# Softplus in a selective-scan kernel: a GpSimd minimum after the log for a VectorE cap before the exp, and the B and C rows copied by ScalarE

## The reference, cut to what matters

```python
def _ssm(h, in_w, xproj_w, dt_bias, A_log, Dskip, out_w):
    xz = h @ in_w
    xs, z = jnp.split(xz, 2, axis=-1)
    xs = jax.nn.silu(xs)
    proj = xs @ xproj_w
    dt = jax.nn.softplus(proj[..., :D_INNER] + dt_bias)
    Bm = proj[..., D_INNER:D_INNER + D_STATE]
    Cm = proj[..., D_INNER + D_STATE:]
    A = -jnp.exp(A_log)
    def step(hst, ins):
        dt_t, B_t, C_t, x_t = ins
        dA = jnp.exp(dt_t[:, :, None] * A)
        hst = hst * dA + (dt_t * x_t)[:, :, None] * B_t[:, None, :]
        y_t = jnp.einsum('bds,bs->bd', hst, C_t)
        return (hst, y_t)
    ...
```

## Time and profile before

| what | value |
|---|---|
| median of three runs | 3235.7 us (3233.97 to 3251.95) |
| span of the profiled execution, first to last instruction | 3238.7 us |
| time of the profiled execution beyond that span | not listed by itself |
| PE, DVE, ACT, POOL busy | 98%, 85%, 84%, 76% of the span |
| rows of the scan | 4 sequences of 128 rows |

### The profile page before, as it was taken

One profiled execution on the slowest core, in us unless ns is written; L12 is line 12 of the kernel. 1 busy time (PEld: TensorE's weight loads), 2 busy tenths in 40 slices (PEclk: granted clock), 3 DMA queues, 4 the chain that ended last, 5 costly groups with the idle time before them and its releaser, 6 DMA issues.

```text
span 3238.7 us, 59471 instructions
## 1 busy us (share of the span) xinstructions
PE 3165.7 (98%) x23272; PEld 2625.2 (81%) x23272; DVE 2754.9 (85%) x3077; ACT 2711.7 (84%) x4528; POOL 2447.2 (76%) x621
## 2 busy tenths in 40 slices
PE   7999999999999999999999999999999999999999
PEld 6998899884699889987479989998648998888844
DVE  3999999966399999996549999999656999999862
ACT  4999999955599999994569999999357999999744
POOL 2999999950199999994039999999305999999800
PEclk9999999999999999999999999999999999999999
DMA  5222322210222222220022222223002222222100
GB/s 187 72 87 68 89 68 84 87 42 1 74 66 87 79 85 74 80 88 30 9 75 72 88 83 74 86 69 92 15 14 79 84 77 84 69 74 81 48 14 7
DMA packets 194232, 222.02 MB, mean 69 GB/s; under 512 B 77336, under 2 KB 149016, under 8 KB 193056
## 3 DMA queue, kind: packets, MB, share of 16 engines
q1 hardware_dynamic: 193952, 218.22, 21.9%
HBM read 213.70 MB, written 4.48 MB: 67 GB/s over the span
## 4 chain that ended last, share of the span: by engine, by line
PE 82%; POOL 8%; issue 4%; DVE 3%; ACT 1%; DMA 1%; SPq 0%; DVEq 0%; ACTq 0%; POOLq 0%
PE bank L1053 22%; PE bank L1033 17%; PE bank L1034 10%; PE bank L933 7%; POOL states L627 5%; PE bank L1029 4%; PE bank L1252 4%; PE bank L1125 3%; POOL y_gated L627 3%; PE bank L1273 2%; PE bank L1285 2%; PE bank L1171 2%; PE bank L1352 2%; DVE states L1509 1%; PE bank L1060 1%
## 5 line engine op out<-in xcount | busy, mean ns | idle before, releaser
L627 POOL TENSOR_TENSOR states<-states,c_rows 128x2048 f32<-128x2048 f32 x336 | 1532.8, 4582 | 411.8 <-DVE states L1509 396.2
L1509 DVE TENSOR_TENSOR_SCAN states<-decay,bank 128x512 f32<-128x512 f32 x1376 | 1576.7, 1201 | 126.1 <-PE bank L1034 111.1
L780 ACT ACTIVATE decay<-dt,a_log 128x512 f32<-128x512 f32 x2048 | 1305.4, 710 | 0.0
L771 ACT ACTIVATE inflow_tok<-dtx_tok,b_tok 128x512 f32<-128x512 f32 x1536 | 995.5, 712 | 69.9 <-PE bank L1034 61.0
L1033 PE MATMUL bank<-ident,inflow_tok 128*128 128x128 f32 x5280 | 904.4, 280 | 36.6 <-DVE states L1509 18.1
L1053 PE MATMUL bank<-ident,states 128*128 128x128 f32 x5504 | 825.2, 273 | 4.4 <-DVE y_gated L1515 3.0
L1509 DVE TENSOR_TENSOR_SCAN y_gated<-decay,bank 128x512 f32<-128x512 f32 x672 | 776.3, 1201 | 12.9 <-ACT decay L780 5.5
L627 POOL TENSOR_TENSOR y_gated<-y_gated,c_rows 128x2048 f32<-128x2048 f32 x168 | 770.0, 4584 | 19.9 <-DVE y_gated L1509 18.1
L1033 PEld LDWEIGHTS bank<-ident,inflow_tok 128*128 128x128 f32 x5280 | 599.1, 141 | 207.6 <-issue 90.4
L1034 PE MATMUL bank<-b_diag,dtx_tok 128*128 128x128 f32 x3520 | 681.0, 275 | 0.0
L1053 PEld LDWEIGHTS bank<-ident,states 128*128 128x128 f32 x5504 | 645.3, 142 | 11.3 <-DVE y_gated L1515 5.3
(11 more groups left out here) (166 smaller groups left out, 2513.1 us busy)
## 6 DMA issues: line engine op xcount, KB each, us to landing
c_rows<-c_spill SPq DMA_DIRECT2D x256, 512.0 KB, 3.7
b_diag<-diag_ring SPq DMA_DIRECT2D x256, 128.0 KB, 2.2
xproj_w<-in_xproj_w SPq DMA_DIRECT2D x32, 320.0 KB, 3.9
in_w<-in_in_w SPq DMA_DIRECT2D x16, 512.0 KB, 4.6
in_w<-in_fc_w SPq DMA_DIRECT2D x8, 512.0 KB, 4.5
xproj_w<-in_w SPq DMA_DIRECT2D x8, 512.0 KB, 4.6
xproj_w<-in_fc_w SPq DMA_DIRECT2D x4, 1024.0 KB, 4.8
x_ahead<-in_x SPq DMA_DIRECT2D x4, 512.0 KB, 6.4
```

Source lines behind the costliest of these rows:

```text
L627: pool.tensor_tensor(state_row, state_row, c_row.to_broadcast([P, KI, L]), ALU.mult).then_inc(weighed, PAIRS)
L771: last_tok = act.activation(inflow_tok[:, r % SLOTS, t, :], dtx_tok[:, d, t, :], ACT.Copy, scale=b_tok[:, d, t, s:s + 1])
L780: act.activation(decay[:, r % SLOTS * KI + k, :], dt[:, d, k, :], ACT.Exp, scale=a_neg[:, d, k, s:s + 1]).then_inc(decay_ready, 1)
L1509: dve.tensor_tensor_scan(state_slots[r % STATES][:, k, time], decay[:, slot, time], banks[k % INFLOW_BANKS][:, time], 0.0, ALU.mult, ALU.a ...
```

## The change

DVE's cap in front of the exp and DVE's copy of the B and C rows are taken out. ACT copies the rows (one instruction of 512 columns behind row 26) and takes the exp straight from PSUM, with the bias as the instruction's own; the log follows in the same row. POOL then bounds the log from above with a minimum in place, one instruction of 512 columns behind rows 32, 38, 42 and 46, and the maximum on DVE, whose place in rows 33, 34, 39, 43, 47 and 48 stays, now waits for that minimum. The semaphore dt_capped is signalled by POOL in place of DVE.

```diff
-DT_CAP = 30.0
+DT_CAP = 40.0
 C_COPY_AT = 26
-C_COPY_REST_AT = 27
-DT_CAP_AT = (30, 36, 40, 44)
-DT_CAP_REST_AT = (31, 37, 41, 45)
-DT_EXP_AT = (32, 38, 42, 46)
-DT_LOG_AT = (33, 39, 43, 47)
+DT_EXP_AT = (31, 37, 41, 45)
+DT_LOG_AT = (31, 37, 41, 45)
+DT_CAP_AT = (32, 38, 42, 46)
 DT_READY_AT = (33, 39, 43, 47)
 DT_READY_REST_AT = (34, 39, 43, 48)
 DTX_AT = (34, 40, 44, 48)
...
@@ gpsimd, prepare
+                if s in DT_CAP_AT:
+                    k = DT_CAP_AT.index(s)
+                    pool.wait_ge(dt_log, n * KI + k + 1)
+                    pool.tensor_scalar(part[:, k, :], part[:, k, :], DT_CAP, None, ALU.min).then_inc(dt_capped, 1)
@@ scalar, prepare
+                if s == C_COPY_AT:
+                    act.wait_ge(c_mm, n + 1)
+                    act.activation(bc_t[:], guest[0], ACT.Copy).then_inc(c_t_ready, 1)
...
-                    act.wait_ge(dt_capped, n * KI + k + 1)
-                    act.activation(part[:, k, :], part[:, k, :], ACT.Exp).then_inc(dt_exp, 1)
+                    act.wait_ge(dt_mm, n * KI + k + 1)
+                    act.activation(part[:, k, :], guest[(k + 1) % 2], ACT.Exp, bias=dt_b[:, d, k:k + 1]).then_inc(dt_exp, 1)
@@ vector, prepare
-                    last = dve.tensor_copy(bc_t[:, c], guest[0][:, c])
...
-                            dve.wait_ge(dt_log, n * KI + k + 1)
+                            dve.wait_ge(dt_capped, n * KI + k + 1)
                         last = dve.scalar_tensor_tensor(dt[:, d, k, c], guest[(k + 1) % 2][:, c], dt_b[:, d, k:k + 1],
                                                         part[:, k, c], ALU.add, ALU.max)
...
-                            dve.wait_ge(dt_mm, n * KI + k + 1)
-                        last = dve.tensor_scalar(part[:, k, c], guest[(k + 1) % 2][:, c], dt_b[:, d, k:k + 1], DT_CAP,
-                                                 ALU.add, ALU.min)
```

More of the change, by code:

```diff
@@ L804, in batch @@
                     if d == 0 or not last:
+                        if s == C_COPY_AT:
+                            act.wait_ge(c_spilled, (b * 2 + d + 1) * 16)
                         prepare(b * 2 + d + 1, 1 - d, s)
@@ L1456, in prepare @@
                         last.then_inc(in_ready, 1)
[L1457 to L1460, removed]
-                    last = dve.tensor_copy(bc_t[:, c], guest[0][:, c])
-                    if s == C_COPY_REST_AT:
-                        last.then_inc(c_t_ready, 1)
                 for k in range(KI):
@@ L1472, in prepare @@
                             last.then_inc(dt_ready, 1)
-                    if s in (DT_CAP_AT[k], DT_CAP_REST_AT[k]):
-                        c = part_of(s, DT_CAP_AT[k], DT_CAP_REST_AT[k])
-                        if s == DT_CAP_AT[k]:
-                            dve.wait_ge(dt_mm, n * KI + k + 1)
-                        last = dve.tensor_scalar(part[:, k, c], guest[(k + 1) % 2][:, c], dt_b[:, d, k:k + 1], DT_CAP,
-                                                 ALU.add, ALU.min)
-                        if s == DT_CAP_REST_AT[k]:
-                            last.then_inc(dt_capped, 1)
             def look_ahead(b, s):
@@ L1526, in _ @@
                     dve.tensor_scalar(scale_cap[:], scale_mul[:], MAX_SCALE_MUL, None, ALU.min).then_inc(cap_ready, 1)
-                if s == DT_CAP_AT[0]:
+                if s == DT_READY_AT[0]:
                     dve.wait_ge(ssm_loaded, 16 * len(SSM))
@@ L1544, in batch @@
                             dve.wait_ge(skip_summed, (b * 2 + d) * KI + TANH_AT.index(s) + 1)
-                        if s == C_COPY_AT:
-                            dve.wait_ge(c_spilled, (b * 2 + d + 1) * 16)
                         prepare(b * 2 + d + 1, 1 - d, s)
```

## The result

The changed kernel takes 3418.7 us (median of four runs, 3416.96 to 3420.13) against 3234.8 us for the kernel before (now the median of four runs), a ratio of 1.0549 (95% interval 1.0528 to 1.057): 184 us slower. The forecast was 143 us slower, 3379, in a range of 3320 to 3430.

A forecast was written before the change was run, and what follows sets the result against it. In the softplus rows POOL was taken to bound first halves and PE second halves. Stretches 127.5 us, DVE's relief -3, first preparation 4 and clock 14 gave 143 on 3235.7: 3379 us, range 3320 to 3430.

The forecast's parts named there:

- What bounds the kernel: Scan rows: four engines within 2% of the wall; softplus rows: POOL without a gap in first halves, PE pacing second halves.
- What is removed is worth little: DVE loses 35.6 us of caps and copies, at most 31 inside scan rows; -3 us taken, bounds -6 and 0.
- ACT's additions are hidden: ACT's eight copies of about 0.58 us fit under its free time, 5 us in all otherwise; exp from PSUM costs nothing.
- The minimum costs 1.75 us: POOL's one-input minimum of 512 columns takes 1.75 us, 1.70 on POOL's clock; ends 0.5 and 2.44.
- Its place: Behind POOL's weigh, the minimum makes DVE's maximum wait at least 4.2 us and POOL idle 3.03 or 3.29; stretch 90.9 us.
- First preparation: Before the scan, the minimum replaces the cap in the chain and ACT's copy of B comes later: 0 to 5 us, 4 taken.
- Nothing is given back after row 47: In the rows after row 47 no lost time is regained; bounds 2 us a half, -14 in all, and 0.
- The clock: After each wait PE may run slow matmuls worth 0 to 1.8 us; 0.5 taken, 14 us in all, bounds 0 and 50.
- rival (b): The clock takes its full price after each PE wait, 1.8 us: 36 us more, 3415; chance 0.15.
- Rival (a): POOL's minimum is cheap, 0.5 us in place of 1.70, and the waits shrink: 34 us less, 3345; chance 0.20.
- (c): The minimum is in time for DVE's maximum and only DVE's relief is left: 3205 us; chance 0.03.
- (d): DVE's wait exists but DVE, PE and ACT make it good behind it, time within 0.5%; chance 0.04.

The follow-up runs named there:

- changed, short filler: The changed kernel with seven small matmuls of zeros on PE behind the last tile of rows 33, 39, 43 and 47: 3383.3 us, ratio 1.0449.
- one column, same place: The changed kernel with POOL's minimum on one column of the tile in place of 512, its place kept: 3365.8 us, ratio 1.0392.
- one row earlier: The changed kernel with the minimum behind rows 31, 37, 41 and 45 in place of 32, 38, 42 and 46: 3277.0 us, ratio 1.0104.
- two rows earlier: The changed kernel with exp, log and the whole minimum behind rows 30, 36, 40 and 44: 3275.5 us, ratio 1.0111.
- two rows earlier, one column: The changed kernel with exp, log and minimum behind rows 30, 36, 40 and 44, the minimum on one column of 512: 3238.1 us, ratio 0.9992.
- no minimum: The changed kernel with POOL's minimum left out, DVE's maximum waiting for the log itself: 3239.0 us, ratio 0.9985.
- the copy alone: The kernel before with only the copy of the B and C rows moved from DVE to ACT: 3238.6 us, ratio 0.9986.

## Why the prediction held in direction and was 40 us short

The place was the right mechanism, and the term of the clock was too small. The stretch from weigh 32 to weigh 47, added up over the seven halves from the starts of the weighs in each trace:

| kernel | stretch, seven halves, us | against before | whole kernel against before |
|---|---|---|---|
| before | 509.0 | | |
| changed | 670.0 | +161.0 | +183.8 |
| changed, short filler | 636.7 | +127.7 | +146.5 |
| one column, same place | 618.8 | +109.8 | +128.9 |
| one row earlier | 531.3 | +22.3 | +34.9 |
| two rows earlier | 530.9 | +21.9 | +38.7 |
| two rows earlier, one column | 508.1 | -0.9 | +1.3 |
| no minimum | 505.7 | -3.3 | -3.1 |

Point by point, with the prediction's own steps:

- **What bounds the kernel.** Held, though POOL and ACT stand 2.6 and 2.7% below the wall in the earlier trace rows, not within 2%. POOL in the first halves has no slack, and the early minimum's price came out of POOL's arithmetic to 0.1 us in the stretch.
- **What is removed is worth little.** Held: -3 us forecast from DVE's freed time. Ahead of the weigh of row 32 the seven halves of the changed kernel are 3.6 us shorter in all, and the kernel with no minimum is 3 us below the one before, which its interval doesn't tell from none.
- **ACT's additions are hidden.** Held; the copy alone costs nothing, and exp from PSUM with its bias doesn't show.
- **The minimum costs 1.75 us.** It took 1.494, and 1.43 to 1.46 on POOL's clock. Worth 28 x 0.25 = 7 us of the sum. By the Trainium skill (GPSIMD Engine Reference, section 4.1, "Engine selection") a one-input operation goes at about line rate, 0.43 us by the prediction's estimate; the trace doesn't agree, 1.494 us is measured.
- **Its place.** Held, but for PE's idle time, which was forecast at about 4 us a wait and is 5.0 on average. The rest: waits of DVE 28 times, 4.8 us on average and 134 us in all (4 to 6 and about 130 forecast), first gaps of 2.93 and 3.20 (3.03 and 3.29). Without its three second gaps, the stretch of the changed kernel is 96.7 - 2.90 - 1.72 - 2.23 = 89.9 us in the half shown, and 95.1 - 1.94 - 1.51 - 1.94 = 89.7 in the first half of that sequence; 3 x (89.7 - 71.6) + 4 x (89.9 - 73.5) = 120 us, against the forecast's 127.5. The minimum's price is nearly all of that difference.
- **First preparation.** The first weigh starts at 81.1 in place of 76.0 us: +5, where +4 was taken. The size is luck. The longer chain, for which the 4 us were taken, costs 0.3: PE's transposes behind the last maximum begin at 61.90, and in the earlier trace rows at 61.60. Most of the rest is the clock's. PE idled for 4.01 us ahead of them, then stands at 0.50 until about 74 us (before, it was back at 1.00 by 66), and the next sixteen matmuls take 3.42 us. With the change:

```profile
61.90 3.81 PE L1010 MATMUL bank<-ident,part 128*128 128x128 f32 x16 [4.01 <-DVE dt L1470]
65.50 3.42 PE L904 MATMUL bank<-silu_cond,y_gated 128*128 128x4 f32 x16
```

and before:

```profile
65.12 1.85 PE L896 MATMUL bank<-silu_cond,y_gated 128*128 128x4 f32 x16
```

- **Nothing is given back after row 47.** Held, and there is a further loss there, the fourth second gap.
- **The clock.** This is the step that failed, a term mis-sized for a reason that didn't hold: "most of it falls into PE's lead of two tiles, and I take 0.5, 28 x 0.5 = 14 us (bounds 0 and 50)". The second gaps are 161 - 120 = 41 us inside the stretches, and behind row 47 the seven halves are 13 us longer: 54 us, 1.9 a wait, just outside the bound. (Some 2 of them would be there at full clock too, by the gaps of 0.25 us and less that the short filler leaves.) What was wrong is the lead. At the moment when PE can begin again, the third scan has just used up one of the two filled banks. What covers PE is the fourth scan alone, 1.2 us, and a tile with its sums at half speed takes longer than that (1419.46 to 1421.40, 1.94 us), row 34 having four of them. Times added up over windows of 1 us from 60 to 3190 us show the same: PE is at 0.50 for 201 us in 34 stretches, against 41 us in 8 before and 72 us in 14 with the short filler.

Together: 120 + 54 + 5 - 3.6 = 175 of the 178 us by which the two spans differ; the remaining 3 lie behind the last weigh and were not traced. The figure measured lies where rival (b) put it, 3415, and its mechanism, the full price of the clock after each wait, was the right one. Its 1.8 us a wait measured 1.9, and the place term under it came out 7 us smaller. That the two lie so close is in part luck: the 1.8 was what one slow stretch of some 3 us cost PE ahead of the first row, while behind row 33 of the half shown PE loses 6.32 - 3.40 = 2.9 us (the last section has the two times), of which the fourth scan hides a part. Rival (a) fell with the price of the minimum; (c) and (d) fell with the waits, of which none was made good.

No version here is faster than the kernel before by more than some tenths of a per cent; the copy alone is the only one whose interval lies below 1, by 0.05 to 0.24%. With place and price taken away the time comes back to it and not measurably below (0.9979 to 1.0005): DVE's relief is worth next to nothing where POOL and PE pace the rows.

## What to carry to other kernels

An instruction in a strictly ordered queue can cost what stands ahead of it in that queue, and not only its own time: here a 1.5 us minimum cost 184 us, 128 of them even when it did almost no work, because it stood behind a 4.5 us weigh and its reader came 2.3 us later. Ask for each added wait where its producer stands, and put it as many rows ahead as its operands allow; what is left then is its busy time, if its engine has no slack. When a wait leaves TensorE idle for some microseconds, add the slow matmuls behind it, and count the lead as it stands at the restart, not as it stood ahead of the wait.

## What the runs showed of the hardware

- On POOL the one-input minimum of 128x512 took 1.494 us and the two-input product of the same size 1.285 us. One operand less didn't make it cheaper. With one column it took 0.219 us, so 2.5 ns for each further column, against the 2.98 that the prediction drew from 4 and 128 columns.
- PE's clock fell to 0.50 with idle times of 3.73 and 3.33 us in the midst of a stretch in which PE is otherwise always busy, stayed full after 0.56 and 2.43, and after 2.80 fell from the second tile on. The length of the idle time alone doesn't decide it: after 2.43 us the clock was at 0.50 in the run with the short filler (matmuls from 2000.13 us on), and after 3.26 us it stayed at 1.00 in the run with one column (from 2768.19 us on).
- Behind the wait of row 33 in the half shown of the changed kernel the slow stretch is about 6 us long: three tiles with their sums took 1425.78 - 1419.46 = 6.32 us, where three took 3.40 at full clock ahead of the wait (1410.75 to 1414.15).
